# A graph layer's front written out in full with its constants behind the first norms, and both additions of an attention gather behind its weighting

## The reference, cut to what matters

```python
xn = _layernorm(x, axis=-1)
# graph attention, 8 heads of 64
h = einsum('ni,hio->nho', xn, W)
s_src = einsum('nho,ho->nh', h, a_src);  s_tgt = einsum('nho,ho->nh', h, a_tgt)
e = leaky_relu(s_src[src] + s_tgt[tgt], 0.2)
ex = exp(e - segment_max(e, tgt)[tgt])
alpha = ex / (segment_sum(ex, tgt)[tgt] + 1e-16)
out = segment_sum(h[src] * alpha[:, :, None], tgt)       # then @ Wo + bo, elu
# linear attention, 8 heads of 32
q = elu(xn @ Wq.T) + 1;  k = elu(xn @ Wk.T) + 1;  v = xn @ Wv.T
context = einsum('bhnd,bhne->bhde', k, v)                # and the sum of k
x = x + gat(xn) + linear_attention(xn)
```

## Time and profile before

| what | value |
|---|---|
| median of the three runs | 2885.69 us (2878.69 to 2886.76) |
| the profiled execution, its own time | 2852.97 us |
| its span | 2850.8 us |
| mean granted TensorE clock | 0.911 |
| TensorE busy | 2189.6 us (77%), weight loads 1390.9 us |
| VectorE busy | 1522.6 us (53%) |
| ScalarE busy | 700.8 us (25%) |
| GpSimd busy | 851.5 us (30%) |

### The profile page before, as it was taken

How to read it: one execution, slowest core, us unless ns; L and a number is a source line. 1 busy time by engine, 2 the same in 40 slices (tenths; PEclk the granted TensorE clock), 3 DMA queues, 4 the chain that set the end, 5 groups by cost and what they waited for, 6 DMA issues and landing times. The chain is left out here.

```text
span 2850.8 us, 33290 instructions
## 1 busy us (share of the span) xinstructions
PE 2189.6 (77%) x9696; PEld 1390.9 (49%) x9696; DVE 1522.6 (53%) x3022; ACT 700.8 (25%) x1795; POOL 851.5 (30%) x879
## 2 busy tenths in 40 slices
PE   0299996888888885699668466777766685999998
PEld 0065653333343445566435255555555574555555
DVE  6977665666767652433254466666666682111111
ACT  0011111111111112133123243434333132222322
POOL 2000003656565630255300355555555100000000
PEclk9999997999999996699889789999888895999999
DMA  1111112323232356133310466666666302000001
GB/s 43 35 74 59 74 59 80 87 73 87 81 89 83 89 60 209 23 60 57 74 50 37 123 171 175 176 177 187 169 180 175 69 8 83 1 0 0 0 1 36
DMA packets 112634, 236.00 MB, mean 83 GB/s; under 512 B 22425, under 2 KB 66860, under 8 KB 109801
## 3 DMA queue, kind: packets, MB, share of 16 engines
q0 software_dynamic: 56784, 160.68, 22.2%
q1 hardware_dynamic: 55704, 73.57, 7.6%
HBM read 193.62 MB, written 40.57 MB: 82 GB/s over the span
## 5 line engine op out<-in xcount | busy, mean ns | idle before, releaser
L2182 PE MATMUL p_ag<-rows_g,oh_g 128*128 128x260 f32 x1488 | 439.9, 438 | 196.7 <-DVE rows_g L2096 103.8
L608 POOL DMA_INDIRECT rows<-h_table,row_rel x372 | 357.7, 962 | 659.1 <-SPq L531 438.9
L2051 POOL DMA_INDIRECT rows_g<-g_table,row_src x372 | 351.8, 946 | 467.0 <-POOLq L95 195.2
L2182 PEld LDWEIGHTS p_ag<-rows_g,oh_g 128*128 128x128 f32 x1488 | 279.0, 208 | 232.6 <-issue 183.1
L860 PE MATMUL p_agg<-rows,oh 128*128 128x256 f32 x744 | 204.0, 408 | 36.0 <-DVE x L659 26.2
L2473 DVE SCALAR_TENSOR_TENSOR x<-p_yf,cw,x 128x256 f32<-128x256 f32 (+1 forms) x160 | 66.3, 477 | 306.4 <-PE p_yf L2564 306.4
L2079 DVE TENSOR_TENSOR acc<-acc,p_ag 128x520 f32 x186 | 128.7, 692 | 168.8 <-PE p_ag L2182 101.1
L2096 DVE TENSOR_TENSOR rows_g<-rows_g,p_n 128x2048 f32<-128x2048 f32 x93 | 212.0, 2279 | 0.0
L860 PEld LDWEIGHTS p_agg<-rows,oh 128*128 128x128 f32 x744 | 134.8, 195 | 106.0 <-issue 50.0
L728 DVE TENSOR_TENSOR fT<-a_sb,p_sel 128x512 f32<-128x512 f32 x200 | 129.0, 684 | 102.8 <-PE p_sel L908 47.7
L2564 PE MATMUL p_yf<-f,h_f 128*128 128x256 f32 (+1 forms) x640 | 145.3, 380 | 0.8 <-ACT h_f L2505 0.8
(11 more groups left out here) (433 smaller groups left out, 3381.1 us busy)
## 6 DMA issues: line engine op xcount, KB each, us to landing
h_table<-h_out SPq DMA_DIRECT2D x20, 1024.0 KB
where_g<-d_table SPq DMA_DIRECT2D x93, 128.0 KB
w<-in_L_ffn_W SPq DMA_DIRECT2D x16, 512.0 KB, 9.5
rows<-h_table,row_rel POOLq DMA_INDIRECT x372
rows_g<-g_table,row_src POOLq DMA_INDIRECT x372
g_table<-row SPq DMA_DIRECT2D x20, 260.0 KB
f<-in_L_ffn_W SPq DMA_DIRECT2D x16, 256.0 KB
x_acc<-x SPq DMA_DIRECT2D x1, 2560.0 KB
```

The lines of the kernel that those rows point to most:

```text
L608: pool.indirect_dma_start(rows[:, r, j], None, st.h_rows, bass.IndirectOffsetOnAxis(ap=st.row_rel[:, at:at + 1], axis=0)).then_inc(gathere ...
L2051: pool.indirect_dma_start(rows[:, r, j], None, st.g_table, bass.IndirectOffsetOnAxis(ap=st.row_src[:, at:at + 1], axis=0)).then_inc(gather ...
L2182: last = pe.matmul(p_a[:, k % 2, h, 0:HALF], oh[:, r, j], rows[:, r, j, h * HALF:(h + 1) * HALF], start=j % SUP == 0, stop=j % SUP == SUP - 1)
```

## The change

In `front1` every loop is written out over the 20 tiles. VectorE takes the reciprocal and two norms first; the block of `iota_p`, constants and `w_a` follows. TensorE waits for `wa_ready` only before the matmuls with `w_a` of tile 0, transposes the next tile between the q product and the context product, and forms the context product of the tile before; the cleared tiles and the counts added ahead go. On VectorE the norm of t+2 stands between `take` and `features`, and the addition of the context of t-1 after them. SP issues each store without waiting for the one before; `row_stored` becomes two semaphores, and VectorE and ScalarE wait on them before they write a row buffer again. The clearing of `acc` goes from VectorE in `attend` to GpSimd in `front1`. In `attend` both additions of batch s-1 stand behind the weighting of batch s.

```diff
@@ front1, SP @@
-            sp.sem_inc(row_free, 2)
-            with sp.Fori(0, T // 2) as i:
-                for u in range(2):
-                    t = 2 * i + u
-                    hold(sp, h_copied, t + 2, held)
-                    hold(sp, s_taken, t + 1, held)
-                    sp.dma_start(st.g_table[ds(t * P, P), :], row[:, u]).then_inc(row_stored, 16)
-                    sp.wait_ge(row_stored, (t + 1) * 16)
-                    sp.sem_inc(row_free, 1)
+            for t in range(T):
+                sp.wait_ge(h_copied, t + 1)
+                sp.wait_ge(s_taken, t + 1)
+                sp.dma_start(st.g_table[t * P:(t + 1) * P, :], row[:, t % 2]).then_inc(row_stored[t % 2], 16)
...
+        @block.gpsimd
+        def _(pool):
+            pool.memset(st.acc[:, :], 0.0).then_inc(acc_cleared, 1)
+            pool.wait_ge(acc_cleared, 1)
@@ front1, VectorE @@
+            dve.wait_ge(sd_ready, 1)
+            link(dve.reciprocal(rstd[:, :], sd[:, :]))
+
+            def norm(t):
+                if t >= 2:
+                    dve.wait_ge(transposed, t - 1)
+                dve.tensor_scalar(xn[:, t % 2], st.x[:, t * D:(t + 1) * D], mean[:, t:t + 1], rstd[:, t:t + 1],
+                                  ALU.subtract, ALU.mult).then_inc(xn_ready, 1)
+
+            def take(t):
+                u = t % 2
+                dve.wait_ge(kv_ready, t + 1)
+                if t:
+                    dve.wait_ge(exp_ready, t)
...
+                if t >= 2:
+                    dve.wait_ge(row_stored[u], 16 * (t // 2))
...
+            norm(0)
+            norm(1)
             link(dve.tensor_tensor(diag_p[:, :], st.ident[:, :], st.iota[:, :], ALU.mult))
             link(dve.tensor_reduce(st.iota_p[:, :], diag_p[:, :], AX, ALU.add))
+            link(dve.memset(live[:, :], 1.0))
+            link(dve.tensor_copy(live[:, T - 1:T], st.rowmask[:, :]))
+            link(dve.memset(context[:, :, :], 0.0))
+            link(dve.memset(st.cb[:, :, :], 0.0))
+            link(dve.memset(ones[:, :], 1.0))
             dve.wait_ge(w_in, 64)
...
-            norm(0, 0)
-            norm(1, 1)
-            with link.loop(T // 2 - 1, 4) as i:
-                for u in range(2):
-                    norm(2 * i + 2 + u, u)
-                    take(2 * i + u, u)
-            for u in range(2):
-                take(T - 2 + u, u)
-            add_context(T)
+            for t in range(T):
+                take(t)
+                if t + 2 < T:
+                    norm(t + 2)
+                features(t)
+                if t:
+                    add_context(t - 1)
+            add_context(T - 1)
@@ front1, ScalarE @@
-            with act.Fori(0, T // 2) as i:
...
+            take_x(0)
+            for t in range(T):
+                if t + 1 < T:
+                    take_x(t + 1)
+                act.wait_ge(neg_ready, t + 1)
+                nc.scalar.activation(neg[:, t % 2], neg[:, t % 2], ACT.Exp).then_inc(exp_ready, 1)
+                act.wait_ge(h_ready, t + 1)
+                if t >= 2:
+                    act.wait_ge(row_stored[t % 2], 16 * (t // 2))
+                nc.scalar.copy(row[:, t % 2, 0:HF], p_h[:, :]).then_inc(h_copied, 1)
@@ front1, TensorE @@
-            pe.wait_ge(wa_ready, 1)
...
+            turn(0)
+            for t in range(T):
+                pe.wait_ge(xT_ready, t + 1)
+                halves = [xT[:, t % 2, k * P:(k + 1) * P] for k in range(K)]
+                if t:
+                    pe.wait_ge(kv_used, t)
+                for k in range(K):
+                    last = pe.matmul(p_kv[:, :], halves[k], w_kv[:, k], start=k == 0, stop=k == K - 1)
+                last.then_inc(kv_ready, 1)
...
+                if t == 0:
+                    pe.wait_ge(wa_ready, 1)
+                for k in range(K):
+                    last = pe.matmul(p_q[:, D:D + 2 * H], halves[k], w_a[:, k], start=k == 0, stop=k == K - 1)
+                last.then_inc(q_ready, 1)
+                if t + 1 < T:
+                    turn(t + 1)
+                if t:
+                    context_product(t - 1)
+                if t:
+                    pe.wait_ge(h_copied, t)
+                for k in range(K):
+                    last = pe.matmul(p_h[:, :], halves[k], w_h[:, k], start=k == 0, stop=k == K - 1)
+                last.then_inc(h_ready, 1)
+            context_product(T - 1)
@@ attend, VectorE @@
-            link(dve.memset(st.acc[:, :], 0.0))
             scores(0)
...
-                if s:
-                    add_sum(GR * (s - 1), tiles[0])
                 weigh(s)
                 if s:
-                    add_sum(GR * (s - 1) + 1, tiles[1])
+                    for g in range(GR):
+                        add_sum(GR * (s - 1) + g, tiles[g])
                 tiles = tiles_of(s)
```

More of the change, by code:

```diff
@@ L1655, in front1 @@
         w_in = sem("w_in1")
-        held = sem("held1")
         dv = sem("dv_front1")
@@ L1674, in front1 @@
         c_used = sem("c_used1")
-        row_stored = sem("row_stored1")
-        row_free = sem("row_free1")
+        row_stored = [sem(f"row_stored{u}") for u in range(2)]
         ends_ready = sem("ends_ready1")
@@ L1710, in _ @@
             sp.wait_ge(z_stored, 16)
+            for u in range(2):
+                sp.wait_ge(row_stored[u], 16 * (T // 2))
             sp.wait_ge(place_stored, 48)
+        @block.gpsimd
+        def _(pool):
+            pool.memset(st.acc[:, :], 0.0).then_inc(acc_cleared, 1)
+            pool.wait_ge(acc_cleared, 1)
         @block.vector
@@ new lines, in features @@
+            def features(t):
+                u = t % 2
+                dve.wait_ge(exp_ready, t + 1)
+                dve.scalar_tensor_tensor(out=k_f[:, u], in0=p_kv[:, 0:D], scalar=0.0, in1=neg[:, u, 0:D],
+                                         op0=ALU.max, op1=ALU.add).then_inc(kv_used, 1)
+                dve.scalar_tensor_tensor(out=st.qT[:, t * D:(t + 1) * D], in0=p_q[:, 0:D], scalar=0.0, in1=neg[:, u, D:],
+                                         op0=ALU.max, op1=ALU.add).then_inc(q_used, 1)
@@ L1719, in _, with add_context @@
+            def add_context(t):
+                dve.wait_ge(c_ready, t + 1)
+                if t:
+                    dve.wait_ge(c_used, t)
+                dve.tensor_tensor(context[:, :, :], context[:, :, :], p_c[:, :, 0:D + 1], ALU.add).then_inc(c_used, 1)
+            norm(0)
+            norm(1)
             link(dve.tensor_tensor(diag_p[:, :], st.ident[:, :], st.iota[:, :], ALU.mult))
             link(dve.tensor_reduce(st.iota_p[:, :], diag_p[:, :], AX, ALU.add))
+            link(dve.memset(live[:, :], 1.0))
@@ L1729, in _ @@
             dve.sem_inc(wa_ready, 1)
[L1730 to L1767, removed]
@@ L1852, in _, with turn @@
             pe.wait_ge(w_in, 64)
-            pe.wait_ge(wa_ready, 1)
             pe.wait_ge(place_ready, 1)
-            pe.sem_inc(transposed, 2)
-            def context_product(t, u):
+            def turn(t):
+                pe.wait_ge(xn_ready, t + 1)
+                if t >= 2:
+                    pe.wait_ge(xT_ready, t - 1)
+                for k in range(K):
+                    last = pe.transpose(p_t[:, t % 2, k * P:(k + 1) * P], xn[:, t % 2, k * P:(k + 1) * P], st.ident[:, :])
+                last.then_inc(transposed, 1)
@@ L1895, in _ @@
-            context_product(T, T % 2)
+            turn(0)
[7 more added lines that the diff above has]
+                last.then_inc(kv_ready, 1)
+                if t:
+                    pe.wait_ge(q_used, t)
+                for c in range(2):
+                    for k in range(K):
+                        pe.matmul(p_q[:, c * P:(c + 1) * P], w_q[:, k, c * P:(c + 1) * P], halves[k], start=k == 0, stop=k == K - 1)
+                if t == 0:
[5 more added lines that the diff above has]
+                    turn(t + 1)
+                if t:
+                    context_product(t - 1)
+                if t:
+                    pe.wait_ge(h_copied, t)
+                for k in range(K):
+                    last = pe.matmul(p_h[:, :], halves[k], w_h[:, k], start=k == 0, stop=k == K - 1)
+                last.then_inc(h_ready, 1)
```

64 lines of the change are left out of this document (17 added, 47 removed).

## The result

The kernel before took 2882.93 us (2878.69 to 2886.76, four runs), the changed one 2811.0 us (2805.9 to 2812.59, four runs): ratio 0.9748, 95% interval 0.9727 to 0.9768, 72 us less. The forecast was 2806.0. The profiled execution of the changed kernel took 2811.01 us.

The account below looks back on a forecast made before the run. Bounds: the gather's weighting-product-addition loop of 5.3 us, disturbed by late-release and half-clock pairs, and the front's table-load stalls. Terms -5.3 - 19.8 - 55 = -80 us from 2852.97: 2773 profiled, 2806 as median; range 2752 to 2872.

Parts of the forecast that it names:

- Norms ahead of the constants: Second layer's front: two norms before the constants block on VectorE start the second tile earlier, gaining 5.3 us.
- The loop written out: Front's tile loop: 6.04 us a tile instead of 7.14, one table load left, gaining 19.8 us.
- The stores and the clearing: Front: SP's stores without waits and acc cleared on GpSimd instead of VectorE; each forecast at zero.
- the two readings in the prediction: GpSimd's fill beside VectorE's statistics: a plain port lock costs 8.8 us; a lock only against two-port forms costs nothing.
- Both additions behind the weighting: Gather stage: a disturbed pair of iterations costs 3.4 us instead of 6.0, for 21 pairs, gaining 55 us.
- The pair with the half clock: Gather stage, new order: two iterations with TensorE at half clock take 12.4 us, 2.1 over.
- The first rival: Gather stage: late releases multiply with full-rate transfers, returning all but 0 to 20 us; 2860 us, chance 0.25.
- The clock rival: Gather stage: shorter TensorE idle keeps the clock, a pair costs 1.3 us; 2762 us, chance 0.20.
- The slower case: Gather stage: releases over 10.2 us make a pair outweigh the old cost and front's gain; 2947 us, chance 0.06.
- The carried difference: Whole kernel: the 32.7 us between profiled execution and median of three runs was carried over unchanged.

Follow-up runs that it names:

- x_more_where: Changed kernel with each batch's 128 KB of one-hot positions loaded a second time into a buffer nothing reads; 2797.54 us.
- with the pause: Changed kernel with each batch's gathers waiting for VectorE's additions six batches back, not only TensorE's releases; 2849.08 us, ratio 0.9792 on a chip with late releases.

## Why the prediction was right, and where its terms were off

**Norms ahead of the constants**, forecast 5.3 us: block start to the second tile's product is 25.06 us against 29.91, 4.85 less. The new norm stands at 1459.72 with the weights' block behind it, as worked out; the one remaining table load is not free, though. In VectorE's timeline:

```profile
1459.72 0.74 DVE L1726 TENSOR_SCALAR xn<-x,mean,rstd 128x256 f32<-128x256 f32 x2
1467.72 0.69 DVE L1773 TENSOR_REDUCE w_a<-wa_t 128x8 f32<-128x512 f32 x1
1472.35 0.42 DVE L1747 SCALAR_TENSOR_TENSOR k_f<-p_kv,neg 128x256 f32<-128x256 f32 x1 [1.96 <-ACT neg L1838]
```

The first tile's k_f waits 1.96 us for Exp and its 1.28 us load.

**The loop written out**, forecast 6.04 us a tile and 19.8 in all: measured 5.82 a tile (18 tiles from 1472.92 to 1577.60) and 23.8 from the second tile to the last context product. TensorE's timeline of one tile:

```profile
1542.73 1.88 PE L1878 MATMUL p_kv<-w_kv,xT 128*128 128x512 f32 x4
1544.45 1.05 PE L1884 MATMUL p_q<-xT,w_q 128*128 128x128 f32 x8
1545.34 0.52 PE L1888 MATMUL p_q<-w_a,xT 128*128 128x16 f32 x4
1545.71 0.41 PE L1860 MATMUL p_t<-ident,xn 128*128 128x128 f32 x2
1545.96 1.03 PE L1868 MATMUL p_c<-v_m,k_f 128*128 128x257 f32 x4
1546.83 1.88 PE L1897 MATMUL p_h<-w_h,xT 128*128 128x512 f32 x4
1548.55 1.88 PE L1878 MATMUL p_kv<-w_kv,xT 128*128 128x512 f32 x4
```

The mechanism was right; the term was mis-sized because I added 0.30 us for two transposes, while the row's 0.41 overlaps its neighbours: the context product starts 0.25 after them. In these rows TensorE alone sets the tile.

**The stores and the clearing**, forecast zero: SP shows no wait for a store, and the fill runs beside the statistics. GpSimd's only instruction of the front, and the statistics by line (ns: least, median, most):

```profile
1447.86 8.77 POOL L1711 MEMSET acc<- 128x10400 f32 x1 [13.15 <-POOLq L95]
...
L104 DVE BATCH_NORM_STATS2 stats<-x x20: 426/427/429, 1448.2 to 1457.6; - x20
```

8.77 us against my 8.8, and 427 ns per statistic as alone. By the Trainium skill, "SBUF — State Buffer", section "Who interferes with whom", a GpSimd fill, which only writes, is locked out only by VectorE's two-port forms. This pair did not interfere, so of the two readings in the prediction the one by forms holds.

**Both additions behind the weighting**, forecast 55 us: 36. This is the term that failed in size, and in more than one place. The loop over two batches was right: behind a late release the next two weightings take the second addition's start plus 5.21 us, where I had 5.2. But I put the release itself, 6.35 us, where that start belongs. Both halves arrive together and VectorE adds one after the other: 1705.29 and 1706.20 in the rows above, 6.5 and 7.45 us after the product's start. So the two intervals from 1695.73 to 1708.40 are 12.67 us (median of 23 such pairs 12.65), not 11.5. The pair with the half clock was nearly right: 12.0 us as a median, where the next late release is four or five batches away, against 12.4.

Two more things hid this. My sum took the new order's 11.5 and 12.4 over 10.3 us for two quiet iterations (3.4), but the old order's 16.6 over 10.6 (6.0); over 10.6 the new one was worked out at 2.7 to 2.8, and the gain at 21 x 3.3 = 68 us, not 55. And "quiet iterations at 5.3" are scarce: 13 of 91 intervals are under 5.5 us, against 36 before. The cost is spread over three or four iterations, not a pair.

As an average: weightings come every 6.27 us, 0.97 over the quiet 5.3, times 91 is 88 us, over 24 runs of eight 3.7 us each. The forecast, counted over 5.3, was 21 times 2.75, or 58. Of the 30 us between them some 20 are the price and some 11 the three more runs of eight. Why there are 24 is not shown; a faster loop alone does not explain it, since x_more_where has a loop of 6.16 us and 19 runs. By the typical profiles the old order pays about 7.1 for each of 18 or 19 runs (654.9 and 657.8 us), the new one 3.7 to 3.8 for each of 24 (613.3 and 616.6).

**The first rival** had this direction (more late releases in a faster loop) but a cause that the runs do not support (transfers at full rate) and far too large a size: over 30 were needed. **The clock rival** is refuted on these chips: a pause of 3.09 us still costs the clock, and the stage has 0.88. On the other chips the clock is 0.98 with the usual pauses of about 1 us per batch. The late release is the usual way to a drop, but not the only one: of 22 drops in the changed kernel's steady part 20 come behind a late release, and two behind pauses of 1.88 and 1.82 us without one. The first:

```profile
1723.69 1.14 PE L2184 MATMUL p_ag<-rows_g,oh_g 128*128 128x260 f32 x4 [1.88 <-issue]
1724.75 2.08 PE L2184 MATMUL p_ag<-rows_g,oh_g 128*128 128x260 f32 x4
```

The Trainium skill's request for no long idle gaps ("TensorE: Matmul & The Clock Gate", "Why this matters for your kernels") agrees with the 3.09 us and with the other chips; these two short pauses it does not explain. **The slower case** needed releases of 10.2 us; the longest that VectorE waited for in the new order's steady part is 6.7, and 7.5 with the pause; the longest that GpSimd waited for, in products at half clock, is 7.6. The one exception is the start of the changed kernel's stage, where the first product's second half is let go 10.8 us after the start (1624.89 to 1635.67), 4.8 us after the 24th gather's end.

**The carried difference.** I read the 32.7 us between profile and median as constant. It was not spread over the kernel: the profiled execution had an unusually quick first layer's gather (550.6 us against 564 to 579 in seven other profiles on chips with late releases). The changed kernel's profile has 574.2 there, so the profiles alone differ by only 42 us where the stages I changed give 65. The sum of the stages, 29.1 + 36.2, is 65; the medians differ by 72 because the profiled gather stage before was itself some 5 to 8 us quicker than the typical one. The forecast of 2806 came out 5 us low: the front gave 4 more than its term, the gather stage 19 less in the profile and 10 to 13 less against a typical run (654.9 and 657.8 against 613.3 are 42 and 45). That it came so near is in part luck: with old and new order counted over the same quiet iterations my own terms give 68 us for the gather stage instead of 55, so a forecast of 2793, 18 us too low.

## What to carry to other kernels

Where one late release disturbs a loop, work that does not need it belongs between its issue and the wait, even when the quiet iteration gains nothing; but count the disturbances anew, since their number can change with the order: 18 to 21 runs of eight became 24 here. Before a sum is made against one profile, compare its untouched stages with a second execution. And measure on more than one chip: here the same change is worth 2.5% on one and 1.2% on another, and the profiles point to half of it removing a wait that only some chips have.

## What the runs showed of the hardware that I had not expected

Two groups of chips: 2875 to 2896 us and 2658 to 2668 us for the kernel before. Each group of runs was on one chip at one time, so the chip and the time are not told apart. For the changed kernel the whole difference, 179 us, lies in two gather stages, and the quicker chips transfer more in them (218 against 182 GB/s). On the slower ones TensorE's releases come together 1.7 to 2.1 us after GpSimd's eighth gather in a row; on the quicker ones a run of 164 gathers holds nothing back. At the start of the gather stage with half the bytes, TensorE's own instructions also come slowly, while 24 gathers are issued. Its timeline there:

```profile
1615.71 0.68 PE L2187 MATMUL p_ag<-rows_g,oh_g 128*128 128x260 f32 x2
1617.95 0.38 PE L2187 MATMUL p_ag<-rows_g,oh_g 128*128 128x260 f32 x1 [1.56 <-issue]
1620.78 0.59 PE L2187 MATMUL p_ag<-rows_g,oh_g 128*128 128x260 f32 x1 [2.45 <-issue]
1623.58 0.17 PE L2170 MATMUL p_n<-node_g,ohT_g 128*128 128x16 bf16 x1 [2.21 <-issue]
1626.38 0.17 PE L2170 MATMUL p_n<-node_g,ohT_g 128*128 128x16 bf16 x1 [2.63 <-issue]
1628.48 0.17 PE L2170 MATMUL p_n<-node_g,ohT_g 128*128 128x16 bf16 x1 [1.93 <-issue]
```

One matmul every 2.1 to 2.8 us, waiting for nothing that the profile shows, until 4.3 us after the end of the 24th gather (1624.3). What connects GpSimd's issue with TensorE here stays open.
